# Rows scattered to expert regions batch by batch, and expert output added into the residual rows, in a mixture-of-experts layer

## The chip, the cores and the metric

The kernel runs on one core of a Trainium2 chip, as one program. The metric is the time on the device in microseconds. Two times are told apart: that of unprofiled runs (their median), and the span of one execution taken by the hardware profiler, on which every row of a view is placed.

## What is computed

The input is x of 8 x 1024 tokens with 256 features, in float32. Two blocks follow one another, each on a layer-normalised x and added back to x:

```
x = x + layernorm(block1(layernorm(x)))     # per-token attention between heads, then an MLP
x = x + layernorm(block2(layernorm(x)))
# block2, on rows h: causal attention with 16 heads over the 1024 tokens of a batch, then
h      = clip(h + attention @ Wo, -100, 100)
flat   = rmsnorm(h, ln2_w)                             # 8192 rows of 256
probs  = softmax(flat @ Wr)                            # 8 experts
topv, topi = top_k(probs, 2);  topv = topv / sum(topv)
o_e    = (silu(flat @ Wg[e]) * (flat @ Wu[e])) @ Wd[e] # Wg, Wu: 256 x 512, Wd: 512 x 256
out    = clip(h + sum over the two experts of topv * o_e, -100, 100)
```

## The kernel before

The program has two parts. `attention_kernel` (lines 83 to 1271) runs a loop of eight iterations, one for each batch, on all engines at once. Tokens are in tiles of 128 rows, 8 tiles to a batch (NT), 64 in all (TT). A batch has three phases; at the end every engine counts itself in (`end_batch`, line 293), SP clears all semaphores one by one (line 360) and lets the four engines go.

- In phase 1, Pool forms for each tile the outer products of keys and values (`work<-QK,VS`, line 434, two halves for a tile), PE sums them over the heads (line 1070), ACT copies the sums to KVS, and DVE (13 heads) and Pool (3 heads, `q_share`, line 397) multiply them with the queries (line 207); DVE reduces (lines 815 and 818). Then the MLP, the layer norms and the rotary embedding. Pool's list of work is fixed: products of tile t, share of tile t - 1, gain of tile t - 3 (`gain2`, line 423). After phase 1 Pool has nothing more to do in the batch.
- In phase 2 there are the scores, the maxima and the weighted values of the attention.
- In the last phase DVE forms H2 (the residual rows) and FL (= flat, in the tile AT), PE the router's logits, and DVE finds the two best experts of each token with `max` and `max_index` (line 1004) and puts expert numbers and shares into ROUTE (lines 1007 to 1015). SP stores x1 (the residual of the second addition, line 340), h2 (line 352), flat (354) and route (356), the latter behind the semaphore `topk`, and waits for all of them before it clears the semaphores.

`experts_kernel` (line 1274) has three blocks, each closed by a barrier of the engines.

- `route_tokens` (1296) loads the routes of all tokens and the 12 MB of expert weights (line 1334). Counts and running sums give each (token, choice) pair a slot; the slots of an expert are padded to whole tiles, 136 tiles in all. Then 64 x 2 pairs of one-hot matrices, made on DVE (lines 1411 to 1413) and multiplied on PE (line 1435), turn the slots into `source`, the list of the tokens in each tile, and `texp` holds the expert of each tile.
- `run_experts` (1444) loops over the 136 tiles, eight to an iteration. Pool gathers 128 rows of flat with an indirect DMA (1498) up to four tiles ahead; PE turns the tile (1575), does the two projections (1584), turns the gated activations (1611) and projects down (1620). ACT does silu and two evacuations (1526, 1531, 1542), DVE the gate (1554) and the copy of the result to Y (1567), and SP stores Y to scratch_y in slot order (1488). DN is one PSUM bank, Y has two buffers.
- `combine` (1626) works in 16 blocks of four tiles. For each, SP loads x1 and h2, Pool gathers the two expert rows of every token (8 indirect DMAs, line 1688) by the slots, DVE multiplies by the shares and adds (1726), clips (1729), takes the statistics (1732, 1736), ACT the root and the normalisation (1704, 1707), DVE adds x1 (1744), and SP stores the output.

A `Signal` counts what was signalled so far; `settle` waits for that count.

## Time and profile before

| | us |
|---|---|
| median of 3 runs | 4459.59 (4457.14 to 4460.53) |
| span of the profiled execution | 4458.2 |
| batches (8) | 0 to 3330.2 |
| routing | 3330.2 to 3457.2 |
| expert loop | 3457.2 to 4251.7 |
| combination | 4251.7 to 4458.2 |

| engine | busy us | share |
|---|---|---|
| PE | 3281.8 | 74% |
| DVE | 2525.6 | 57% |
| ACT | 1616.7 | 36% |
| POOL | 1256.7 | 28% |

The busy shares are means over stages with different limits, so the page alone doesn't say what bounds the kernel. The slices show where the stages are, the windows give each stage's own busy times, and the timeline shows who releases whom. In a row of the timeline, the part in brackets is the engine's idle time before it and what ended it. Times of issue and landing of DMAs are in a view of their own.

### The profile page before, as it was taken

The page shows a single profiled execution, that of the slowest core. Times are in us where ns is not written, and L with a number is a line of the kernel's source. Part 1 is how long each engine was busy: PE and PEld are TensorE (multiplying, and loading weights), DVE is VectorE, ACT ScalarE, POOL GpSimd, SP SyncE. Part 2 cuts the span into 40 slices and gives each one's busy share as a digit, 9 for nine tenths or more (in the row PEclk, how much of TensorE's full clock was granted, in tenths as well). Part 3 has the DMA queues.
Part 4 walks back from the last instruction along what each step waited for, and adds up shares of the span by engine and source line. Part 5 has one row for each costly group of instructions (what it writes and reads, how often), then busy time and mean ns, then how long its engine had stood idle before and what let it go on. Part 6 is the DMA issues. An engine that isn't in the chain of part 4 may idle for free. (4 is left out here: it accounts for less than half of the span.)

```text
span 4458.2 us, 53612 instructions
## 1 busy us (share of the span) xinstructions
PE 3281.8 (74%) x17032; PEld 1909.6 (43%) x17033; DVE 2525.6 (57%) x4655; ACT 1616.7 (36%) x3717; POOL 1256.7 (28%) x873
## 2 busy tenths in 40 slices
PE   6667859775977687587759775976774999999910
PEld 5433623452354235333623452453331666666600
DVE  6764857386658656673857486566749111111156
ACT  2435245433634352444236333624440222222222
POOL 6400910271055008201810460064000111111156
PEclk9889979887988798798879887987885999999955
DMA  1130040004000400310040004002212111111156
GB/s 31 21 52 21 1 71 3 21 0 73 2 20 11 63 21 1 48 25 21 1 72 2 20 1 73 2 20 36 28 45 90 47 45 45 45 45 45 43 182 199
DMA packets 172478, 177.41 MB, mean 40 GB/s; under 512 B 31952, under 2 KB 159696, under 8 KB 172240
## 3 DMA queue, kind: packets, MB, share of 16 engines
q1 hardware_dynamic: 159568, 139.78, 14.6%
q0 software_dynamic: 12672, 34.62, 2.6%
q8 instruction: 130, 2.13, 0.2%
q14 instruction: 108, 0.88, 0.1%
HBM read 106.32 MB, written 67.24 MB: 39 GB/s over the span
## 5 line engine op out<-in xcount | busy, mean ns | idle before, releaser
L434 POOL TENSOR_TENSOR work<-QK,VS 128x2048 f32<-128x2048 f32 x128 | 520.1, 4086 | 1734.7 <-DVE QK L764 1734.2
L925 DVE TENSOR_REDUCE NM<-MX 128x1 f32<-128x128 f32 (+7 forms) x1024 | 735.3, 753 | 448.8 <-PE MX L1162 438.5
L652 ACT ACTIVATE PR<-SP_ 128x512 f32<-128x512 f32 (+3 forms) x1536 | 694.0, 489 | 459.8 <-PE SP_ L1196 312.9
L1160 PE MATMUL MX<-KST,work 96*128 96x512 bf16 (+3 forms) x1536 | 444.8, 354 | 270.9 <-DMA work<-scratch_qd 211.5
L1193 PE MATMUL SP_<-work,KST 99*128 99x512 bf16 (+3 forms) x1536 | 469.6, 333 | 69.6 <-ACT PR L652 32.3
L1554 DVE TENSOR_TENSOR AG<-UB,SL 128x512 f32<-128x512 f32 x136 | 94.1, 692 | 500.3 <-PE UB L1584 500.3
L1160 PEld LDWEIGHTS MX<-KST,work 96*128 96x128 bf16 x1536 | 127.3, 103 | 534.8 <-DVE NM L925 225.5
L1209 PE MATMUL OA<-PR,V 128*32 128x512 f32 (+3 forms) x3072 | 327.3, 498 | 3.3 <-ACT PR L652 3.3
L818 DVE TENSOR_REDUCE AT<-work 128x208 f32<-128x3328 f32 x56 | 324.6, 5797 | 0.0
L1070 PE MATMUL OB<-work,ident 128*128 128x256 f32 x1024 | 258.9, 416 | 74.9 <-POOL work L434 74.9
L1531 ACT ACTIVATE SL<-GB 128x512 f32<-128x512 f32 x136 | 81.3, 598 | 602.6 <-PE GB L1584 602.6
L1193 PEld LDWEIGHTS SP_<-work,KST 99*128 99x128 bf16 x1536 | 145.7, 98 | 288.6 <-ACT PR L652 198.5
L1070 PE MATMUL OA<-work,ident 128*128 128x256 f32 x1024 | 238.2, 392 | 40.9 <-POOL work L434 40.9
L1498 POOL DMA_INDIRECT XG<-scratch_flat,index x136 | 129.4, 952 | 492.5 <-PE TX L1575 457.2
L1070 PEld LDWEIGHTS OB<-work,ident 128*128 128x128 f32 x1024 | 212.8, 211 | 119.6 <-issue 83.6
L207 DVE TENSOR_TENSOR work<-QK,KVS 128x3328 f32<-128x3328 f32 x64 | 263.5, 4117 | 0.0
L1584 PE MATMUL GB<-wg,XTm 128*128 x544 | 257.8, 596 | 0.3 <-issue 0.3
L1620 PE MATMUL DN<-wd,AGT 128*128 x1088 | 257.1, 379 | 0.8 <-ACT AGT L1542 0.8
L1584 PE MATMUL UB<-wu,XTm 128*128 x544 | 256.0, 593 | 0.0
L1620 PEld LDWEIGHTS DN<-wd,AGT 128*128 128x128 f32 x1088 | 206.6, 190 | 86.6 <-issue 65.5
L1162 PE MATMUL MX<-mask_qk,identb 128*128 128x128 bf16 x1024 | 236.5, 233 | 0.0
L1070 PEld LDWEIGHTS OA<-work,ident 128*128 128x128 f32 x1024 | 196.3, 195 | 81.0 <-issue 43.4
(242 smaller groups left out, 5252.7 us busy)
## 6 DMA issues: line engine op xcount, KB each, us to landing
work<-scratch_qd SPq DMA_DIRECT2D x96, 256.0 KB, 9.4
scratch_y<-Y SPq DMA_DIRECT2D x136, 128.0 KB, 1.7
scratch_qd<-work SPq DMA_DIRECT2D x48, 256.0 KB, 7.7
X<-in_L_attn_x SPq DMA_DIRECT2D x8, 1024.0 KB, 5.7
scratch_x<-X SPq DMA_DIRECT2D x8, 1024.0 KB, 16.2
scratch_h<-A SPq DMA_DIRECT2D x8, 1024.0 KB, 4.6
scratch_flat<-AT SPq DMA_DIRECT2D x8, 1024.0 KB, 6.2
XH<-scratch_x SPq DMA_DIRECT2D x16, 512.0 KB, 4.3
```

Of the source, the lines that this page charges most:

```text
L207: return eng.tensor_tensor(dst.rearrange("p (h e d) -> p h e d", e=HD, d=HD), QK[:, u % 3, h0 * HD:h1 * HD].rearrange("p (h e) -> p h e", ...
L434: sg["prod1"].by(pool.tensor_tensor(P1[t % 2][:, i * hh * D:(i + 1) * hh * D].rearrange("p (h e d) -> p h e d", h=hh, e=HD), QK[:, t % 3, ...
L652: sg["exp"].by(act.activation(PR[:, n % 8, q0:512], SP_[:, n % 2, q0:512], ACT.Exp))
L818: sg["attn"].by(dve.tensor_reduce(AT[:, u, 0:c0].rearrange("p (h d) -> p h d", d=HD), P2[:, 0:(H - POOL_HEADS) * D].rearrange("p (h e d) - ...
L925: sg["mx"].by(dve.tensor_reduce(NM[:, qt, h:h + 1], src, AX.X, ALU.max, negate=True))
L1070: m = pe.matmul(OAB(u)[:, 0:D], ident[:, :], P1[u % 2][:, h * D:(h + 1) * D], start=h == 0, stop=h == H - 1)
L1160: m = pe.matmul(out, lhsT, KST[0:MROW, g, k0:k1], start=True, stop=not last)
L1162: m = pe.matmul(out[:, k1 - k0 - P:k1 - k0], identb[:, :], mask_qk[:, :], start=False, stop=True)
L1193: m = pe.matmul(SP_[:, n % 2, q0:512], KST[0:KROWS, g, kt * P:(kt + 1) * P], QST[0:KROWS, g * G + h, c * 512 + q0:(c + 1) * 512], start=Tr ...
L1209: m = pe.matmul(OA[32 * h:32 * (h + 1), q0:512], V1[:, kt, g, :], PR[:, (G * k + h) % 8, q0:512], start=kt == 0, stop=last, tile_position= ...
L1584: m = pe.matmul(out[:, s % 2], XT[:, s % 2, c * P:(c + 1) * P], w[:, bass.ds(e, 1), c, :].squeeze(1), start=c == 0, stop=c == FC - 1)
L1620: m = pe.matmul(DN[:, 0:D], AGT[:, s % 2, c * P:(c + 1) * P], wd[:, bass.ds(e, 1), c, :].squeeze(1), start=c == 0, stop=c == FK - 1)
```

## The change

The route and flat tensors in DRAM, the lists, the gathers and the scratch_y tensor go. The parts:

1. FL becomes the first 256 columns of a tile FX with rows of 260 values: the row, the number of the first choice, the difference of the two shares, the second share, and the row's number in h2. FX, SLOT and `count` live through both parts of the program. x1 and h2 are laid out so that a partition's rows are contiguous in DRAM; h2 has 128 spare rows.
2. At the end of each batch, DVE builds the one-hots of the two choices, PE sums them with two float32 matmuls of 64 columns, and DVE forms each pair's row in a DRAM tensor xs with a region for each expert, and keeps the running count. The store of the route and that of flat go.
3. At the start of the next batch Pool issues 16 indirect DMAs that scatter the rows of FX (1040 bytes each) to xs, ahead of its other work. In the first iteration they write to spare rows. DVE waits for them before it writes FL again. The scatters of the last batch stand in the routing block.
4. `plan_tiles` takes the place of `route_tokens`: from the eight counts it forms the expert and the first row of each tile, and SP writes 128 padding rows behind each region.
5. In `run_experts`, SP loads each tile with a plain DMA whose row comes from a register, four tiles ahead. DVE works out each row's share from the row itself and multiplies it in with the evacuation. Pool adds the tile to h2 with an indirect DMA that accumulates, and waits for each before the next. x1 is loaded into SBUF in 16 pieces meanwhile.
6. `finish` takes the place of `combine`: no gathers; h2 in blocks of four tiles with four buffers, the clip on Pool, and two blocks between statistics and addition on DVE.

The setup uses a part of `work` for the raw weights and has 12 more Pool instructions and one more DMA.

```
             with pool.Fori(0, B) as b:
+                for t in range(NT):
+                    for j in range(2):
+                        pool.indirect_dma_start(
+                            out=dram["xs"], out_offset=bass.IndirectOffsetOnAxis(ap=SLOT[:, j, t:t + 1], axis=0),
+                            in_=FX[:, t, :], in_offset=None).then_inc(scattered, 16)
...
-                sp.wait_ge(sg["fl"].sem, NT)
-                st_.by(sp.dma_start(fld[bass.ds(b, 1)].squeeze(0), FL[:, :, :]), 16)
-                sp.wait_ge(sg["topk"].sem, 1)
-                st_.by(sp.dma_start(routed[bass.ds(b, 1)].squeeze(0), ROUTE[:, :, :]), 16)
...
+                    if c == 0:
+                        dve.wait_ge(scattered, (b + 1) * (2 * 16 * NT))
...
+                for j in range(2):
+                    ds.by(dve.tensor_tensor(M[:, j], ioe[:, :].unsqueeze(1).broadcast_to(sh),
+                                            topi[:, :, j:j + 1].broadcast_to(sh), ALU.is_equal))
+                sg["onehot"].by(dve.tensor_tensor(BR[:, :, :], M[:, 0], M[:, 1], ALU.add))
...
+                dve.wait_ge(sg["sums"].sem, 1)
+                ds.by(dve.tensor_copy(tot[:, :, :], MX[:, 1, 1, 0:NT * E].rearrange("p (t e) -> p e t", e=E)))
+                ds.by(dve.tensor_tensor_scan(cum[:, :, :].rearrange("p e t -> p (e t)"), ...
...
+                sg["slots"].by(dve.tensor_copy(SLOT[:, :, :], slotf[:, :, :]))
...
+                pe.wait_ge(sg["onehot"].sem, 1)
+                pe.matmul(MX[:, 1, 0, 0:NT * E], below[:, :], choices, start=True, stop=True)
+                sg["sums"].by(pe.matmul(MX[:, 1, 1, 0:NT * E], ones[:, :], choices, start=True, stop=True))
...
 (plan_tiles, SP and Pool)
+            sp.wait_ge(sg["const"].sem, 5)
+            sp.wait_ge(sg["ends"].sem, 1)
+            for e in range(E):
+                row = sp.value_load(endi[0:1, e:e + 1], min_val=0, max_val=E * REGION)
+                sg["padded"].by(sp.dma_start(dram["xs"][bass.ds(row, P), :], pad[:, :]), 16)
+            sg["padded"].settle(sp)
...
+            for t in range(NT):
+                for j in range(2):
+                    sg["scattered"].by(pool.indirect_dma_start(... in_=FX[:, t, :] ...), 16)
...
 (run_experts, SP, Pool and DVE)
+            def load(s, n):
+                row = sp.value_load(at, min_val=0, max_val=E * REGION)
+                sp.dma_start(XG[:, s], dram["xs"][bass.ds(row, P), :]).then_inc(sg[f"loaded{s}"].sem, 16)
...
+                    pool.wait_ge(sg["y"].sem, n0 + s + 1 + CREDIT)
+                    if not (first and s == 0):
+                        pool.wait_ge(sg["added"].sem, (n0 + s) * 16)
+                        pool.sem_inc(sg["freed"].sem, 1)
+                    pool.indirect_dma_start(
+                        out=dram["h2"], out_offset=bass.IndirectOffsetOnAxis(ap=XG[:, s, ROW - 1:ROW].bitcast(U32), axis=0),
+                        in_=Y[:, s % 2], in_offset=None, compute_op=ALU.add).then_inc(sg["added"].sem, 16)
...
-                    dve.tensor_copy(Y[:, s % 2], DN[:, 0:D]).then_inc(sg["y"].sem, 1)
+                    dve.wait_ge(sg["freed"].sem, n0 + s - 1 + AHEAD)
+                    dve.tensor_scalar(Y[:, s % 2], DN[:, 0:D], share[:, s, 1:2], None, ALU.mult).then_inc(sg["y"].sem, 1)
...
 (finish)
+            for n in range(NB):
+                sp.wait_ge(sg["out"].sem, (n + 1) * U)
+                sg[f"stored{n % R}"].by(sp.dma_start(od[n], X1[:, n * U:(n + 1) * U, :]), 16)
+                if n + R < NB:
+                    load(n + R)
...
+            for n in range(NB):
+                pool.wait_ge(sg[f"loaded{n % R}"].sem, 16 * (n // R + 1))
+                sg["clip"].by(pool.tensor_scalar(h, h, 100.0, -100.0, ALU.min, ALU.max))
```

## Rows read from the trace of the kernel before

**Rows 1.** The page's slices: mean busy share of the DMA engines, in tenths.

```profile
DMA  1130040004000400310040004002212111111156
```

**Rows 2.** Windows: us, busy time and count by engine, granted PE clock, DMA share, GB/s.

```profile
454.00:563.30 109.30, 89.12 (x356) 70.19 (x356) 93.72 (x46) 24.58 (x68) 102.44 (x32) 0.92 0.00 1
3330.20:3372.00 41.80, 11.74 (x24) 3.25 (x24) 30.10 (x94) 0.00 (x0) 1.45 (x8) 0.50 0.97 304
3372.00:3457.20 85.20, 45.60 (x114) 11.82 (x113) 78.09 (x326) 0.67 (x2) 4.36 (x6) 0.50 0.02 5
3457.20:4251.70 794.50, 793.28 (x2988) 495.05 (x2988) 151.84 (x272) 186.14 (x408) 131.36 (x164) 1.00 0.14 44
4251.70:4458.20 206.50, 0.00 (x0) 0.00 (x0) 128.52 (x402) 48.24 (x88) 133.34 (x160) 0.51 0.64 204
```

**Rows 3.** Timeline, end of the first batch: start, duration, engine, line, out<-in, idle before.

```profile
432.30 0.18 DVE L1007 CAST ROUTE<-topi 128x16 f32<-128x16 uint32 x1
...
433.13 0.17 DVE L1015 TENSOR_TENSOR ROUTE<-tw 128x8 f32<-128x8 f32 x1
```

**Rows 4.** SP's semaphore clears, by source line 360.

```profile
L360 SPq EVENT_SEMAPHORE_RANGE_CLEAR  x736: 25/30/49, 436.6 to 3329.4; - x184
```

**Rows 5.** Timeline, start of the second batch.

```profile
444.83 1.28 ACT L486 ACT_TABLE_LOAD   x1 [12.25 <-issue]
...
454.00 14.54 POOL L434 TENSOR_TENSOR work<-QK,VS 128x2048 f32<-128x2048 f32 x4 [240.48 <-DVE QK L764]
...
468.50 1.50 POOL L207 TENSOR_TENSOR PP<-QK,KVS 128x768 f32<-128x768 f32 x1
...
469.93 3.62 DVE L207 TENSOR_TENSOR work<-QK,KVS 128x3328 f32<-128x3328 f32 x1
```

**Rows 6.** First batch: Pool by source line 434, and its first product in the timeline.

```profile
L434 POOLq MODIFY_POOL_CONFIG  x16: 11/11/11, 24.3 to 2920.5; - x16
...
39.53 7.29 POOL L434 TENSOR_TENSOR work<-QK,VS 128x2048 f32<-128x2048 f32 x2 [32.76 <-DVE QK L764]
```

**Rows 7.** Timeline of the combination, Pool's gathers.

```profile
4256.32 0.95 POOL L1688 DMA_INDIRECT Y<-scratch_y,indexc  x1 [0.30 <-issue]
...
4361.87 1.26 POOL L1688 DMA_INDIRECT Y<-scratch_y,indexc  x1 [0.30 <-issue]
```

**Rows 8.** DMA issues: kernel's tensors, count, KB each, median us to landing.

```profile
scratch_y<-Y SPq DMA_DIRECT2D x136, 128.0 KB, 1.7
...
XH<-scratch_h SPq DMA_DIRECT2D x16, 512.0 KB, 5.5
...
wd<-in_L_ffn_Wd SPq DMA_DIRECT2D x1, 4096.0 KB, 32.1
...
XG<-scratch_flat,index POOLq DMA_INDIRECT x136, 2.7
Y<-scratch_y,indexc POOLq DMA_INDIRECT x128, 3.3
```

**Rows 9.** Timeline, start of the expert loop.

```profile
3455.01 0.69 PE L1575 MATMUL TX<-identm,XG 128*128 128x128 f32 x2 [5.42 <-DMA XG<-scratch_flat,index]
...
3457.17 3.62 PE L1584 MATMUL GB<-wg,XTm 128*128 x4 [0.29 <-issue]
```

**Rows 10.** Timeline, one tile of the expert loop.

```profile
3481.94 0.38 PE L1575 MATMUL TX<-identm,XG 128*128 128x128 f32 x2
...
3483.14 0.94 POOL L1498 DMA_INDIRECT XG<-scratch_flat,index  x1 [4.41 <-PE TX L1575]
```

**Rows 11.** Combination grouped by line: count, busy us, mean ns, idle before.

```profile
L1744 DVE TENSOR_TENSOR XH<-XH 128x256 f32<-128x256 f32 x64 | 27.2, 425 | 13.9 <-ACT XH L1707 10.7
L1732 DVE BATCH_NORM_STATS2 stc<-XH 128x6 f32<-128x256 f32 x64 | 22.5, 414 | 0.5
...
L1736 DVE BATCH_NORM_AGGREGATE mvc<-stc 128x2 f32<-128x6 f32 x64 | 6.1, 157 | 2.4 <-DVE stc L1732 0.5
```

**Rows 12.** Timeline of Pool in phase 1 of the second batch.

```profile
494.23 4.11 POOL L423 TENSOR_TENSOR A<-AT,g2row 128x256 f32<-128x256 f32 x1
```

More of the change, by code:

```diff
@@ L1387, in _ @@
[L1387 to L1393 removed]
+            do(dve.memset(eps[:, :], LN_EPS))
@@ L1416, in _ @@
-            one_hots(0, True)
-            with dve.Fori(1, TT - 1) as t:
-                one_hots(t)
-            one_hots(TT - 1)
-            dve.wait_ge(sg["lists"].sem, 2 * TT)
-            do(dve.tensor_copy(src[:, :, :], pk[:, 0:2 * NS].rearrange("p (x n) -> p x n", x=2)))
-            do(dve.scalar_tensor_tensor(out=src[:, 0], in0=src[:, 1], scalar=float(P), in1=src[:, 0], op0=ALU.mult, op1=ALU.add))
-            do(dve.tensor_copy(source[:, :], src[:, 0]))
-        @block.tensor
-        def _(pe):
-            pe.wait_ge(sg["onehot"].sem, 1)
-            choices = BR[:, :, :].rearrange("p t e -> p (t e)")
-            pe.matmul(pr[:, 0:TT * E], below[:, :], choices, start=True, stop=True)
-            sg["sums"].by(pe.matmul(pt[:, 0:TT * E], ones[:, :], choices, start=True, stop=True))
-            def lists(t, first=False, last=False):
-                for j in range(2):
-                    pe.wait_ge(sg["place"].sem, 2 * t + j + 1)
-                    pe.matmul(pk[:, 0:2 * NS], lane1[:, j], tile1[:, j].rearrange("p x n -> p (x n)"),
-                              start=first and j == 0, stop=last and j == 1).then_inc(sg["lists"].sem, 1)
-            lists(0, first=True)
-            with pe.Fori(1, TT - 1) as t:
-                lists(t)
-            lists(TT - 1, last=True)
@@ L1466, in run_experts @@
         DN = ps("DN", [P, 512])
-        sg = Signals(nc, ctx, "index gathered0 gathered1 gathered2 gathered3 tx xT g gu silu ag tpa agT down y stored0 stored1 moved", "m_")
+        names = "tx xT g gu silu ag tpa agT down y picked share added freed " + " ".join(f"loaded{s}" for s in range(UNROLL))
+        sg = Signals(nc, ctx, names, "m_")
         N = NSLOT_TILES
         U = UNROLL
-        yd = dram["y"]
         block = ctx.enter_context(nc.Block())
@@ L1522, in _ @@
+            pool.sem_inc(sg["freed"].sem, AHEAD)
+            body(0, True)
+            with pool.Fori(1, N // U) as i:
+                body(i * U, False)
+            pool.wait_ge(sg["added"].sem, N * 16)
         @block.scalar
@@ L1644, in combine @@
-        rows = {n: dram[n].rearrange("(i t p) f -> i p t f", t=U, p=P) for n in ("x1", "h2")}
+        HH = sb("HH", [P, R, U, D])
+        st = sb("stc", [P, R, U, 6])
+        mv = sb("mvc", [P, R, U, 2])
+        cf = sb("cfc", [P, R, 3, U])
+        sg = Signals(nc, ctx, "clip stat var std inverse shift norm out " + " ".join(f"loaded{r} stored{r}" for r in range(R)), "c_")
+        hd = dram["h2"][0:B * S].rearrange("(p g) f -> p g f", p=P)
         od = out.rearrange("b (i t p) f -> (b i) p t f", t=U, p=P)
```

433 lines of the change are left out of this document (203 added, 230 removed).

## The prediction

> **What bounds the kernel now.** I read the row of DMA shares in the page's slices first [rows 1], then cut the span into stages by the windows view [rows 2], and then read the two ends of a batch in the timeline [rows 3 to 6]. Eight batches take 0 to 3330 us. Token routing takes 3330.2 to 3457.2: at first the DMA engines are full with the expert weights (share 0.97), then they are idle and a chain on DVE and PE builds the lists. The expert loop takes 3457.2 to 4251.7 with PE busy 793.3 of 794.5 us at full clock: it is bound by PE alone. The combination takes 206.5 us with no PE work; what it waits for is Pool, which issues 128 gathers one after another [rows 7]. In the first phase of a batch both Pool (102.4 of 109.3 us) and DVE (93.7) are nearly full [rows 2], so this phase starts its chain when Pool starts.
>
> I sum in profiled time, span 4458.2 us. The median is 4459.6, so 1.4 us are added at the end. A change within 0.2% (8.9 us) counts as none.
>
> **Routing stage: 70 us less.** The scans over 64 tiles, 128 pairs of one-hots and the list matmuls go. What is late next is the load of the weights. The windows put its end at 3372, 41.8 us after the stage begins (DMA share 0.97 up to there, 0.02 behind it [rows 2]; wd, the last, needs 32.1 us to land [rows 8]). Now 16 scatters of the last batch (2.1 MB) run beside these 12.6 MB; at the window's 304 GB/s [rows 2] they add 7 us, 0 to 7 as bounds, so about 48. The 8 padding rows sit behind the weights on SP's queue; two landings of about 2 us and a block change bring the first tile's load, and from a tile's landing to the first GB matmul it is 2.2 us (PE turns the first tile at 3455.01, GB starts at 3457.17 [rows 9]). Pads 2, block change 1, four loads issued and the first landed 3, then 2.2: the first GB comes 57 us after the stage begins, against 127.0 now. The scatters on Pool (16 at 1.25 us [rows 7], 20 us) and the short DVE plan behind them lie under the weights; without that cover they would cost about 30 us. Gain 70; bounds 60 to 78 (pads that are not held up by the weights).
>
> **Expert loop: nothing, if the scatter-add keeps up.** PE's work for a tile is unchanged, 794.5 us for 136 tiles or 5.84 us each [rows 2]. Two DVE instructions on one column are added beside 5.8 us in which DVE works 1.1 us; the product with the share takes the place of a PSUM copy of equal size; SP loads tiles four ahead (23 us of cover), and the pieces of x1 fill an idle queue (DMA share 0.14 [rows 2]). The open price is Pool's. Each tile is added to h2 by one indirect DMA, and Pool waits for its landing before it issues the next; behind this wait stand the release of Y, so the next Y product and the next DN matmul. No accumulating DMA is in the trace. Bounds: a wait released at 3482.32 (end of TX) leads to an issue at 3483.14, 0.8 us [rows 10]; a gather lands 2.7 us after its issue, 3.3 in the loaded stage, a plain store of 128 KB 1.7 [rows 8]. The lower end is 0.8 + 1.7 = 2.5 us. The upper end doubles a loaded gather and a store in sequence, as if each row were read, added and written in turn: 0.8 + 2 x (3.3 + 1.7) = 10.8. I take one loaded gather and half a store more, 0.8 + 3.3 + 0.9 = 5.0 us, nearer to the gather, which has the same 128 rows and the same issuer. That is 0.8 us below the tile's 5.84, so the loop keeps its 794.5 us. The margin is thin.
>
> The Trainium skill (DMA: Bandwidth & Descriptors, Anatomy of one DMA — SWDGE path) gives a DMA from Pool some 2.0 us fixed, most of it the receipt of the write, plus bytes at 436 GB/s; with one more read of the row the landing would be estimated at about 3.6 us with the instruction's 0.95, and the loop would stay PE-bound with more room. Our gather's 2.7 agrees with the fixed part; no run shows the accumulating form.
>
> **End: 104 us less.** Now the stage from the last Y to the end is 206.5 us [rows 2], paced by 8 gathers per block of four tiles at 1.25 us and more [rows 7]. After: the last scatter-add must land (0.8 + 4.2) and the block changes (2.2 as now), 7.2. A first load of 512 KB lands in 5.5 us [rows 8]; the clip moves to Pool, priced by a Pool instruction with two inputs and 768 columns at 1.50 us [rows 5], so 2.0 for 1024 columns with one input. DVE then does 16 blocks: four statistics 1.41 and four additions 1.70 (22.5 and 27.2 us for 64 [rows 11]), aggregation 0.38 (6.1 us for 64), and root, inverse and shift, three operations in turn on ACT and DVE, some 0.7 together (0.17 to 0.2 each as in [rows 3], and the passing on), 4.2 us in all; Pool and DVE slow each other (256 columns took 4.11 us on Pool beside DVE's product, [rows 12]), so I take 5.0, bounds 4.2 and 7.0. 16 x 5.0 = 80. The last normalisation and addition 4, the last store 3.4. Sum 7.2 + 5.5 + 2.0 + 80 + 4 + 3.4 = 102, gain 104, bounds 72 to 117. The transfers are 16.8 MB; at 304 GB/s 55 us, so they are hidden, just.
>
> The Trainium skill (GPSIMD Engine Reference, Key points) says that GpSimd shares its SBUF interfaces with VectorE and contends with DVE instructions that have two SBUF inputs. The additions here are such; a clip held through each of them would be 3.7 us and still under the 5.0, so the sum would be the same by either.
>
> **Start of each batch: 87 us more.** The scatter of the previous batch stands first in Pool's loop, before the products of tile 0, and is queued ahead of them. The cores are let go at 444.8; Pool's first product starts at 454.00, released by DVE [rows 5], so Pool has 9.2 us of slack. Sixteen indirect DMAs at the 1.25 us of back-to-back gathers [rows 7] take 20.0, and 0.8 to start: Pool is free at 465.6, 11.6 us late. Does this reach the end of the phase? Pool works without a gap from 454.00 on, DVE's first attended product waits until 469.93 for a row of work that begins with Pool's product, and after it DVE is full as well [rows 2, 5]. I find no slack, so the whole 11.6 goes on the path, 7 times: 81. In batch 0 Pool is free at 24.3 and needed at 39.5 [rows 6]: 24.3 + 20.8 = 45.1, 5.6 more. Together 87; bounds 48 (0.95 each, without the 0.30 between) and 127 (1.56 each, as beside DVE [rows 7]).
>
> **End of each batch: 7 us more.** The store of the route and its landing leave the path: DVE's last operation ends at 433.30, the clears start at 436.6 [rows 3, 4], 3.3 us. Against it DVE gets 16 more small operations, from 5 to 21. Five took 1.0 us [rows 3]; some 14 dependent steps at 0.20 to 0.26 and the rest overlapped give 4.9, while PE's two sums of 64 columns lie beside DVE's work on the shares. So +3.9 - 3.3 = +0.6, and two more semaphores of 92 that take 8.2 us to clear, +0.2: +0.8, 8 times 7; bounds -4 and +24. The stores of flat and x1, the setup's extra Pool operations (about 5 us, before PE's start at 16) and FL inside rows of 260 cost nothing: each ends long before what waits for it.
>
> **The sum.** 4458.2 - 70 + 0 - 104 + 87 + 7 = 4378 us, and 1.4 around it: 4380 us, 1.8% less.
>
> **Rivals.** (1) Slower: the scatter-add takes longer than a tile. Then the loop is paced by Pool's wait. With a landing of 6.5 us the chain is 7.3 and the loop costs 136 x 1.46 = 199 more: 4579. It turns the sign from a chain of 5.84 + 80/136 = 6.4 us. For it: the whole operation is absent from the trace and its upper bound is 10.8; against it: the small landings of both of its halves. (2) The scatter at the batch start is hidden, because PE and ACT have work of the next tiles to do meanwhile: 4380 - 87 = 4293. Against it stand the gapless rows of Pool and DVE. (3) Scatters on Pool cost more than gathers, 2 us each, as rows of 1040 bytes: 8 x 16 x 0.75 = 96 more, 4476, slower by 0.4%; nothing in the trace points there. (4) Pool's clip paces the end at 7 us a block: 32 more, 4412, inside my forecast's own range.
>
> **How the numbers follow.** Forecast with its own bounds (4330 to 4440) 0.70, rival 1 0.17, rival 2 0.08, rival 3 0.05. Faster 0.78 (the forecast and rival 2), same 0.04 and slower 0.18 (rivals 1 and 3, a part of them near zero). The range: low 4325, which leaves out rival 2; high 4475, which takes in rival 3 and the mild end of rival 1.
>
> **What would show it.** Scatter-add: the tiles' pace on PE's GB rows stays about 5.8, and Pool waits for DVE's Y, not for a DMA. Batch start: Pool's first product about 21 us after the release, DVE's first attended product 11 to 12 us later than now, and batches some 12 us longer. Routing: first GB 57 us after the stage begins, behind the weights. End: 5 us from block to block, DVE the busiest. I am wrong if the GB pace is above 5.9, if a batch grows by under 8 or over 18 us, or if the last stage takes over 125.

## The result and the profile after

| | us |
|---|---|
| before, median of 4 runs on one chip | 4460.06 (4457.14 to 4463.38) |
| after, median of 4 runs | 4350.69 (4344.27 to 4355.95) |
| ratio | 0.9757, 95% interval 0.9745 to 0.9769 |
| span of the profiled execution, before and after | 4458.2 and 4343.7 |

The changed kernel is 2.4% faster: 109.4 us in the medians, 114.5 us in the spans. Forecast were 4380 us and 1.8%. By stages of the two spans (a stage is taken from the issue of the first weight to the first GB matmul, from there to the last DN matmul, and from there to the end):

| | before | after | difference | forecast |
|---|---|---|---|---|
| batches | 3330.7 | 3409.5 | +78.8 | +94 |
| routing | 126.5 | 50.7 | -75.8 | -70 |
| expert loop | 794.1 | 795.2 | +1.1 | 0 |
| end | 207.0 | 88.3 | -118.7 | -104 |

The windows of the kernel after, to be read beside those of [rows 2] (us, busy time and count of PE, weight loads, DVE, ACT and Pool, granted PE clock, DMA share, GB/s). The first is phase 1 of the second batch from Pool's first product on, then the weights, the expert loop and the end:

```profile
471.79:581.09 109.30, 86.20 (x346) 68.08 (x346) 92.28 (x42) 21.55 (x60) 102.28 (x32) 0.90 0.01 2
3409.51:3451.40 41.89, 0.00 (x0) 0.00 (x0) 8.12 (x19) 0.00 (x0) 16.53 (x22) 0.50 1.00 360
3460.23:4255.44 795.21, 794.45 (x2988) 495.59 (x2988) 194.38 (x543) 186.19 (x408) 210.63 (x135) 1.00 0.32 55
4255.44:4343.70 88.26, 0.01 (x1) 0.00 (x0) 59.08 (x225) 37.47 (x81) 18.22 (x17) 0.51 0.61 193
```

Phase 1 has the same 102.3 us of Pool in 109.3 as before: it is not slower, it is later. The loop is still PE's, 794.45 of 795.21 us at full clock. In the end stage DVE has 59.1 us instead of 128.5.

**A batch's end and start.** The timeline from the last step that both kernels share (`tw`, 432.19 before, 440.28 here) over the last slot number and SP's clears to the second batch (start, duration, engine, line, out<-in, idle before; the row of clears is the view of source line 373):

```profile
440.28 0.15 DVE L1041 TENSOR_TENSOR tw<-top 128x8 f32<-128x8 f32 x1
...
444.48 0.17 DVE L1084 CAST SLOT<-slotf 128x16 uint32<-128x16 f32 x1
...
L373 SPq EVENT_SEMAPHORE_RANGE_CLEAR  x752: 25/30/49, 444.8 to 3407.5; - x188
...
451.60 1.00 POOL L426 DMA_INDIRECT scratch_xs<-FX,SLOT  x1 [232.64 <-issue]
452.84 1.28 ACT L520 ACT_TABLE_LOAD   x1 [12.16 <-issue]
...
471.79 3.68 POOL L468 TENSOR_TENSOR work<-QK,VS 128x2048 f32<-128x2048 f32 x1
```

From `tw` to ACT's release it is 12.56 us, and 12.64 before (432.19 to 444.83 [rows 5]). Slots take DVE until 444.65, where before it ended at 433.30 [rows 3] and SP then waited for the store of the route until 436.6 [rows 4]. From ACT's release to Pool's first product it is 18.95 us, 9.17 before [rows 5]: 9.8 more. DVE's first attended product starts 36.5 us behind the release (489.32), 25.1 before (469.93 [rows 5]). Over the batches 2 to 8 the mean distance of Pool's first products is 423.57 us, 413.20 before.

**Routing.** The stage begins at 3409.51 with the issue of the first weight. Behind it on SP's queue, and the first PE work of the expert loop:

```profile
3416.84 13.47 SPq L1397 DMA_DIRECT2D wd<-in_L_ffn_Wd  x1
3432.17 21.06 SPq L1403 DMA_DIRECT2D scratch_xs<-pad  x8
3456.08 8.79 SPq L1505 DMA_DIRECT2D XG<-scratch_xs  x8
...
3458.14 0.69 PE L1598 MATMUL TX<-identm,XG 128*128 128x128 f32 x2 [59.01 <-DMA XG<-scratch_xs]
...
3460.23 3.78 PE L1607 MATMUL GB<-wg,XTm 128*128 x4 [0.28 <-issue]
```

The weights have landed at 3451.4, 41.9 us after the first issue, as before, although 2.1 MB of scatters ran beside them: the second window above shows share 1.00 and 360 GB/s, against 304 [rows 2]. From there it is 4.7 us to the issue of the first tile's load (3456.08), 2.1 to PE's first transpose and 2.1 to the first GB.

**Expert loop.** Pool's scatter-add by source line 1527 (count: duration in ns min/median/max, its idle time by what ended it, landing), and one tile's Y with Pool behind it in the timeline:

```profile
L1527 POOL DMA_INDIRECT scratch_h<-Y,XG x136: 1556/1561/1637, 3473.4 to 4258.2; - x136
  DVE Y L1590: 522.4, 115
  DMA scratch_h<-Y,XG: 78.1, 18
DMA to landing us min/median/max: 3.6/3.8/5.5
...
3507.52 0.48 DVE L1590 TENSOR_SCALAR Y<-DN,share 128x256 f32<-128x256 f32 x1 [1.06 <-PE DN L1643]
...
3508.82 1.56 POOL L1527 DMA_INDIRECT scratch_h<-Y,XG  x1 [3.75 <-DVE Y L1590]
```

Pool waits for DVE's Y 115 times of 136 and 18 times for its own last DMA. GB follows GB at 5.82 us (median), and with the changes from one expert to the next the loop takes 5.85 us a tile.

**End.** The last scatter-add, the first clip and the statistics behind it, one block further on, and the waits of the stage (us in total, times, longest):

```profile
4258.22 1.56 POOL L1527 DMA_INDIRECT scratch_h<-Y,XG  x1 [2.98 <-DMA scratch_h<-Y,XG]
4268.04 1.04 POOL L1687 TENSOR_SCALAR HH<-HH 128x1024 f32<-128x1024 f32 x1 [8.26 <-DMA HH<-scratch_h]
4269.18 1.41 DVE L1712 BATCH_NORM_STATS2 stc<-HH 128x6 f32<-128x256 f32 x4 [13.21 <-POOL HH L1687]
...
4326.31 1.04 POOL L1687 TENSOR_SCALAR HH<-HH 128x1024 f32<-128x1024 f32 x1 [3.56 <-DMA HH<-scratch_h]
4326.38 0.99 DVE L1725 SCALAR_TENSOR_TENSOR cfc<-mvc,cfc 128x4 f32<-128x4 f32 x1
...
4331.61 1.40 DVE L1712 BATCH_NORM_STATS2 stc<-HH 128x6 f32<-128x256 f32 x4
...
POOL HH L1687 <- DMA HH<-scratch_h: 55.1, 16, 9.4
```

The statistics of the 16 blocks start at 4269.18 to 4331.61, 4.16 us apart in the mean. Pool waits for a load before every clip.

### The profile page after: what moved, and what is told of

Same layout as the page of the kernel before. It is cut to its first block and busy times, and to the rows that moved or that the text cites. A ratio compares the mean times of both kernels' runs of the same rounds, so it can differ in the third digit from the quotient of the medians.

```text
span 4343.7 us, 52684 instructions
## 1 busy us (share of the span) xinstructions
PE 3234.6 (74%) x16932; PEld 1905.7 (44%) x16933; DVE 2419.9 (56%) x4478; ACT 1605.2 (37%) x3710; POOL 1358.4 (31%) x849
## 5 line engine op out<-in xcount | busy, mean ns | idle before, releaser
L426 POOL DMA_INDIRECT scratch_xs<-FX,SLOT x128 | 124.0, 969 | 1678.3 <-issue 1678.0
L1527 POOL DMA_INDIRECT scratch_h<-Y,XG x136 | 212.2, 1560 | 616.2 <-DVE Y L1590 522.4
L1140 PE MATMUL OA<-work,ident 128*128 128x256 f32 x1024 | 252.7, 409 | 105.4 <-POOL work L468 105.4
L1140 PEld LDWEIGHTS OA<-work,ident 128*128 128x128 f32 x1024 | 207.2, 206 | 149.6 <-POOL work L468 81.4
```

What stands on the lines that cost most here:

```text
L1140: m = pe.matmul(OAB(u)[:, 0:D], ident[:, :], P1[u % 2][:, h * D:(h + 1) * D], start=h == 0, stop=h == H - 1)
L1527: pool.indirect_dma_start(out=dram["h2"], out_offset=bass.IndirectOffsetOnAxis(ap=XG[:, s, ROW - 1:ROW].bitcast(U32), axis=0), in_=Y[:, s ...
```

## The experiments

Where the time of a changed kernel is given without an interval, it is that of one execution. The kernel before took 4447.4 to 4473.1 us in seven executions on one chip, so differences of half a percent between such times aren't told apart, and the smaller effects are read from the stages and rows of the traces.

### Where the 16 scatters stand

Theory A was that the 10 us in each batch are Pool's queue and nothing else. From the start of its last gain (line 452) to the start of the rotary embedding it is 34.8 us, nearly all of it idle for Pool, and Pool is idle throughout phase 2. So the scatters were moved into these gaps.

```
             with pool.Fori(0, B) as b:
-                (the 16 scatters)
                 ...
                 sg["ag"].settle(pool)
+                (the 16 scatters)
                 for t in range(NT):
                     pool.wait_ge(sg["q2"].sem, t + 1)
```

> Pool issues the same 16 scatters of the previous batch, not ahead of its products but after its last gain, where it stood idle for 34 us in each batch of the kernel before. Nothing is left out. Theory A (the scatters at the start of a batch push the whole phase 1): Pool's first product comes some 10 us earlier again in each of seven batches and 6.6 us in the first, so the span falls by 70 to 80 us from 4343.7 to about 4268, and the batch period goes back from 423.6 to about 413.5. Rival B (the longer batch comes from the longer end of a batch and the store of the rows, wherever the scatters stand): the period stays above 420 and the span above 4320. Rival C (the scatters hurt DVE or the rotary products where they now stand): period between 415 and 420.

Measured: 4349.53 us, ratio to before 0.9753 (0.9728 to 0.9778), the same as the changed kernel, and not the 4268 of theory A. A batch takes 424.1 us. The start of the batch was free again, yet all of it was lost elsewhere. ACT in the second batch, behind Pool's first scatter of that batch (the last starts at 589.62):

```profile
570.49 0.99 POOL L479 DMA_INDIRECT scratch_xs<-FX,SLOT  x1 [0.28 <-POOL A L452]
...
587.43 0.38 ACT L575 ACTIVATE A2T<-SP_ 128x256 f32<-128x256 f32 x1 [7.44 <-remote]
...
590.92 0.38 ACT L575 ACTIVATE A2T<-SP_ 128x256 f32<-128x256 f32 x1 [3.11 <-remote]
```

PE had ended the transposes that these copies wait for by 584.2 and 588.6. The release reached ACT some 3 and 2 us later, too late for the view to name PE as the releaser ("remote"). Such rows are in every batch, 22 on ACT (79.3 us of idle in all, not all of it delay) and 2 on DVE; the traces of before and after have none. From the last gain to the rotary embedding it is now 43.5 us, 8.7 more. TensorE's clock doesn't begin it. The granted clock is at 1.2 GHz (0.50) for 10.2 us of this stretch, from 587.9 on, where with eight and eight it is at 2.4 GHz; but the first late release of the batch comes before that, at 585.31.

The second run left eight scatters at the start and put eight in the gap:

```
-                for t in range(NT):
+                for t in range(NT // 2):
                     (two scatters, at the start)
                 ...
                 sg["ag"].settle(pool)
+                for t in range(NT // 2, NT):
+                    (two scatters)
```

> Eight of the 16 scatters stand at the start of a batch, eight after Pool's last gain. Nothing is left out. Theory A with a slack: eight take 8 x 1.28 = 10.2 us from Pool's release, which came 1.2 us before ACT's, and Pool's product was needed 9.2 us after ACT's release, 10.4 after its own: the eight fit into the slack, and the period is that with none at the start, 413 to 414, span 4265 to 4275. Rival (each scatter at the start costs its 1.28 us, without slack): the saving is half, period about 418.5, span about 4305.

Measured: 4270.17 us, span 4268.3, a batch 413.9 us. In the second batch:

```profile
449.59 0.97 POOL L426 DMA_INDIRECT scratch_xs<-FX,SLOT  x1 [0.30 <-issue]
451.46 14.53 POOL L468 TENSOR_TENSOR work<-QK,VS 128x2048 f32<-128x2048 f32 x4 [0.90 <-issue]
```

Pool ends its eighth scatter at 450.56, and DVE its operand QK at 451.37, so the product doesn't wait for Pool. The first half of the scatters fits in the slack and the second half in the gap; 75.6 us of the 78.8 by which the batches had become longer are gone (3409.5 and 3333.9). Theory A holds for the start. What was slow with 16 in the gap is a second cost.

### What delays PE's release of ACT

Two runs took apart what the 16 scatters in the gap had and the eight had not: to run beside the transposes of the second half of the MLP (P), or to be many on end (N).

```
 (16 in the gap, a pause until the copies are done)
                 for t in range(NT):
+                    if t == NT // 2:
+                        pool.wait_ge(sg["a2T"].sem, NT)
                     (two scatters)
```

> All 16 scatters stand in the gap before the rotary embedding, but Pool waits after the eighth until ACT has copied the last tile of A2T. In the run with 16 in the gap without this pause, ACT's second group of A2T copies (line 575) came 7.4 and 3.1 us after it was idle, released late, and the batch took 424.1 us, where eight in the gap gave 413.9. Theory P (what is slow is PE's hand-over of these transposes while scatters are in flight): the copies come as in the run with eight, 4.0 and 0.3 us of idle, the batch takes 413 to 415 us and the span is 4260 to 4275. Theory N (it is the number of scatters issued on end, the eleventh and later ones): the pause is of no use or the late releases move to the lines that run beside scatters 9 to 16; a batch takes 420 to 424 us, span 4320 to 4348.

```
 (eight at the start, eight in the gap, but later)
                 sg["ag"].settle(pool)
+                pool.wait_ge(sg["hid"].sem, 1)
                 for t in range(NT // 2, NT):
                     (two scatters)
```

> Eight scatters at the start of the batch and eight in the gap, as in the run of 4270.17 us, but Pool waits with those in the gap until PE has done the first half of the MLP's first product (the semaphore hid), so that they run beside the second group of A2T copies instead of before it. Theory P (PE's transposes hand over late while scatters are in flight): the idle time before these copies grows from 4.0 to 6 or 7 us and from 0.3 to 2 or 3, and a batch takes 418 to 424 us, span 4300 to 4350. Theory N (the number of scatters on end): eight are too few, so the batch stays at 413 to 415 us and the span at 4265 to 4280.

Measured: 4287.79 and 4278.62 us with 4471.54 for one execution of before on that chip (0.959 and 0.957; 0.957 was the ratio of the run with eight and eight). A batch takes 415.5 and 414.5 us. In the later variant the scatters run from 574.22 to 584.10, and ACT's second group of copies lies within them:

```profile
578.58 0.66 ACT L580 ACTIVATE A2T<-SP_ 128x256 f32<-128x256 f32 x2 [4.03 <-PE SP_ L1112]
```

No late release, so P falls: scatters beside these transposes are not enough. With the pause there is no "remote" row either; the copies came before the ninth scatter. But seven releases by PE are 0.6 to 0.7 us late there, six of them to DVE with all second eight issued, one to a copy in the last batch. In the second batch PE ends OB at 592.72 (as a rule the release comes 0.04 us later in this phase), and:

```profile
593.33 0.42 DVE L890 TENSOR_TENSOR O<-OB,A 128x256 f32<-128x256 f32 x1 [0.55 <-PE OB L1179]
```

PE's next instruction, which waits for the same matmuls, starts 0.64 us behind them too. So here eight on end were not wholly without effect. Open was whether a short pause does as well, so in a third run the second eight go beside the copies, behind a pause only as long as the first eight need to land.

```
                     if t == NT // 2:
+                        pool.wait_ge(scattered, (b + 1) * (2 * 16 * NT) - 16 * NT)
+                        pool.sem_inc(sg["drained"].sem, 1)
```

> All 16 scatters in the gap before the rotary embedding, with a short pause: after the eighth, Pool waits until all that it has issued have landed (2 to 3 us), and then issues the other eight, which so run beside the second group of A2T copies. What is to be told apart is what made ACT's copies late in the run with 16 scatters on end, and not where eight ran beside the same copies, nor where Pool paused until these copies were done. Theory D (scatters on end pile something up, and a short pause drains it): no copy is late, 4.0 and 0.3 us of idle before the second group, a batch takes 413 to 417 us, 4270 to 4295. Theory T (the second eight within some 20 us of the first are enough, with or without a short pause): idle of 6 to 8 and 2 to 3 us before these copies, a batch takes 420 to 424 us, 4320 to 4350.

Measured: 4272.05 us, before 4461.9 on that chip, 414.0 us for a batch.

```profile
574.02 0.95 POOL L482 DMA_INDIRECT scratch_xs<-FX,SLOT  x1 [2.28 <-DMA scratch_xs<-FX,SLOT]
...
575.51 0.66 ACT L578 ACTIVATE A2T<-SP_ 128x256 f32<-128x256 f32 x2 [4.03 <-PE SP_ L1110]
576.48 0.66 ACT L578 ACTIVATE A2T<-SP_ 128x256 f32<-128x256 f32 x2 [0.32 <-PE SP_ L1110]
```

A pause of 2.3 us takes all late releases away, and the time with them: theory D's number, though from one execution. How far it proves D has a limit. With 16 on end the first late release of this batch was due when PE ended OB at 583.76, 13.3 us after the first scatter and with 11 of them issued; it reached DVE (line 888) at 585.31. Here the copies were released on time up to 576.48, 14.7 us after the first scatter, but with ten issued. So the time since the first scatter is not the cause; that an eleventh after the pause would have been harmful can't be excluded, because until 587 us ACT and DVE wait for PE no more. What is shown is that in this gap eight on end cost at most the 0.7 us above, that 16 on end cost 8.7 us a batch, and that the same 16 with a pause of 2.3 or 5.6 us in the middle cost little or nothing (0.957 and 0.959 of before, eight and eight 0.957).

That 16 on end are enough by themselves is not so, and the changed kernel shows it. At the start of the second batch its scatters run on end from 451.60, the twelfth starts at 465.69, and yet:

```profile
464.35 1.03 PE L1129 MATMUL MX<-wqkvT,XT 128*128 128x256 f32 x4
...
465.42 0.60 ACT L598 ACTIVATE EX<-MX 128x512 f32<-128x512 f32 x1 [3.12 <-PE MX L1129]
```

PE ends at 465.38 and ACT has its release 0.04 us later. In the seven batches 1 to 7 there is one such release each with 11 to 14 scatters issued, 13.5 to 17.1 us behind the first, and all are on time. So something in the gap of phase 1 is needed besides the number. What it is, and what piles up, no run shows; a scatter lands in 2.5 us (median), so few are under way at a time.

### All 16 in phase 2

```
                 end_phase(pool, 1)
+                (the 16 scatters; none at the start of the batch)
                 end_phase(pool, 2)
```

> All 16 scatters of a batch stand at Pool's start of phase 2, in which Pool has nothing else to do; none at the start of the batch and none before the rotary embedding. Here SP also moves queries and keys through DRAM (DMA share 0.7 over the first 60 us of the phase). Theory A (only Pool's queue at the start of the batch costs something): 4260 to 4275 us. Theory P (PE's transposes hand over late while scatters are in flight; phase 2 has none of that kind): the same, 4260 to 4275. Theory N (scatters beyond the tenth on end delay any release by PE): in phase 2 ACT and PE hand over to each other every half microsecond, so 9 us or more in each batch, 4330 to 4400. A rival of another kind: the 2.1 MB of scatters delay the queries' transfers, which phase 2 waits for (26 us of waits on them in each batch before), by up to 5 us in each batch: 4300 to 4310.

Measured: 4318.10 us, span 4316.2, a batch 420.3 us. Waits of the second batch's phase 2, first of this run, then of the run with eight and eight (us in total, times, longest):

```profile
DVE NM L960 <- PE MX L1233: 61.5, 46, 18.5
PE MX L1231 <- DMA work<-scratch_qd: 31.3, 2, 18.1
```

```profile
DVE NM L965 <- PE MX L1238: 55.0, 44, 15.4
PE MX L1236 <- DMA work<-scratch_qd: 25.8, 2, 13.6
```

The queries' transfers through DRAM come 5.5 us later; that is the rival of another kind, and with it most of the 6.4 us by which a batch is longer than with eight and eight (413.9) is accounted for. Late releases are there too, but few (three of DVE in all batches, 3.0 us, 19.9 to 21.8 us after the first scatter), and cost little, for PE starts its scores 12 us into the scatters and DVE is behind it. Theory A's 4260 to 4275 falls for this place: Pool's gap is free, the DMA engines are not.

### The price of the scatter-add

The loop costs nothing as long as the chain of Pool fits under a tile. One run doubled the operation (each adds half of Y), one took the addition out of it, so that in that one the expert rows overwrite the residual rows.

```
-                    pool.indirect_dma_start(out=dram["h2"], ..., in_=Y[:, s % 2], compute_op=ALU.add)
+                    for k in range(2):
+                        if k:
+                            pool.wait_ge(sg["added"].sem, (n0 + s) * 32 + 16)
+                            pool.sem_inc(sg["turned"].sem, 1)
+                        pool.indirect_dma_start(out=dram["h2"], ..., in_=Y[:, s % 2], compute_op=ALU.add)
```

> Each tile of the expert loop is added to h2 twice, one after the other with a wait for the landing between, each time with half the share; the sum is the same. It doubles the chain of waits on Pool: landing 3.8 us and about 0.7 from the wait to the next issue, so one link is 4.5 and two are 9.0 us a tile. Theory (the scatter-add sets the pace as soon as its chain is longer than PE's 5.85 us): loop of 136 tiles at about 9.0 us, 1225 us in place of 796, span about 4773; Pool waits for its own DMA in each tile. Rival (the accumulating DMAs overlap or the chain hides behind the four tiles of lookahead): loop below 900 us.

Measured: 4838.28 us; forecast were 4773, from links of 4.5 us. By source line 1531:

```profile
L1531 POOL DMA_INDIRECT scratch_h<-Y,XG x272: 1556/1560/1636, 3473.4 to 4749.2; - x136
  DMA scratch_h<-Y,XG: 767.8, 245
```

```profile
3606.68 1.56 POOL L1531 DMA_INDIRECT scratch_h<-Y,XG  x1 [3.05 <-DMA scratch_h<-Y,XG]
3611.24 1.56 POOL L1531 DMA_INDIRECT scratch_h<-Y,XG  x1 [3.01 <-DMA scratch_h<-Y,XG]
```

Now Pool waits for its own DMA nearly always, and one link of the chain is 4.6 us from issue to issue: 3.8 to land and 0.8 to go on. The loop takes 1270.0 us, 9.34 a tile, twice 4.6 and a little; the last stage takes 105.9 us instead of 88.3. So the single chain is 4.6 us under PE's 5.85: 1.2 us of margin, and rival 1's mechanism is real, only its price is not.

```
-                        in_=Y[:, s % 2], in_offset=None, compute_op=ALU.add)
+                        in_=Y[:, s % 2], in_offset=None)
```

> The indirect DMA of the expert loop writes the rows of Y over h2 in place of adding them; what is left out is the addition, so the output holds the expert part of one expert alone. It measures what the accumulating form costs: with it Pool's instruction takes 1.56 us and the landing 3.8. I expect 0.97 us and 2.5 us, as for the scatters to the regions, and no change of the time: PE sets the pace of 5.85 us in both. Rival (the accumulate loads the DMA engines and slows the tile loads or the matmuls): the loop gets shorter by more than 3 us.

Measured: 4345.79 us, span 4343.9, the loop 795.2 us as with the addition. Without it the instruction takes 0.96 us instead of 1.56 and lands in 2.6 us instead of 3.8: the addition costs 0.6 us of Pool and 1.2 us of landing, and nothing here.

### What the missing gathers gave

The kernel before, whose combination gathers for its first two blocks alone:

```
-            with pool.Fori(1, NP) as i:
-                for k in range(2):
-                    gather(i, k)
...
-                    dve.wait_ge(sg[f"gathered{k}"].sem, (i + 1) * 32 * U)
+                    dve.wait_ge(sg[f"gathered{k}"].sem, 32 * U)
```

> The kernel before, whose combination gathers the expert rows for its first two blocks alone; the other 14 blocks add the rows of those two, so that the expert part of the output is left out there. All the rest of the combination stays: loads, shares, clip, statistics, stores. Theory A (Pool's 128 gathers pace the last stage): without them DVE does, with 128.5 us of busy time in it: the stage falls from 206.5 to 135 to 150 us and the time to 4388 to 4404. Rival: the stage is bound by its loads and stores (share 0.64 of the DMA engines) or by the steps in turn of DVE and ACT, and keeps 190 us or more: 4440 or more. In the first case the new form of the addition (87.7 us) would owe some 60 us of its 119 to the missing gathers and the rest to DVE's work that went, in the second nearly all to the order of the blocks.

Measured: 4436.79 us; its last stage takes 175.5 us instead of 207.0, between the two theories. The window of that stage:

```profile
4259.51:4435.00 175.49, 0.00 (x0) 0.00 (x0) 128.49 (x402) 48.24 (x88) 16.24 (x20) 0.51 0.47 156
```

Here block follows block at 9.4 us on DVE (4303.69 and 4313.13 for the start of line 1741), of which it works 8.0 (128.49 / 16). So Pool's gathers did end last in the kernel before, but DVE stood only 2 us a block behind them: 31.5 of the 118.7 us belong to the gathers. DVE's own work fell by 69.4 us (128.49 to 59.08), and the remaining 17.8 are idle time of DVE. That the order with two blocks between statistics and addition closed it is argued: no run changes the order alone.

### The padding rows, and five buffers

```
-            (SP) the eight stores of pad behind the weights
 (Pool) the constants ahead of the last batch's 16 scatters, no longer behind them
+        @block.scalar
+        def _(act):
+            act.wait_ge(sg["const"].sem, 5)
+            act.wait_ge(sg["ends"].sem, 1)
+            for e in range(E):
+                row = act.value_load(endi[0:1, e:e + 1], min_val=0, max_val=E * REGION)
+                sg["padded"].by(act.dma_start(dram["xs"][bass.ds(row, P), :], pad[:, :]), 16)
```

> The changed kernel with the eight stores of the padding rows issued from ACT's queue instead of SP's, where one issue was held for 13.4 us behind the expert weights. Theory A (the pads behind the weights set the first tile's load): in the changed kernel wd lands 41.9 us after the stage begins, the last pad is issued at 43.4, the first tile's load at 46.6 and the first GB matmul comes at 50.7. From ACT's queue the pads land under the weights, so the first load follows the weights alone: the first GB 44 to 47 us after the stage begins, the time 4344 to 4348, 3 to 7 less. Rival: ACT's issue is held just as SP's was, since the DMA engines are full with 12 MB, and the pads land no earlier than before: 50 to 51 us, 4350.

Measured: 4338.49 us, span 4336.6.

```profile
3406.47 8.57 ACTq L1424 DMA_DIRECT2D scratch_xs<-pad  x8
...
3412.67 17.60 SPq L1397 DMA_DIRECT2D wd<-in_L_ffn_Wd  x1
3434.64 19.10 SPq L1508 DMA_DIRECT2D XG<-scratch_xs  x8
...
3453.18 3.77 PE L1610 MATMUL GB<-wg,XTm 128*128 x4 [0.29 <-ACT XTm L1543]
```

The stage begins at 3404.60, so the first GB comes 48.6 us after it, 2.1 less. ACT's queue issued all eight in 8.6 us while SP's issues of wu (3405.06 to 3412.62) and wd were held, so the rival falls. The gain is less than expected since the first XG load is itself behind the weights now: the load stage is the weights' alone. The rest of the 7 us lies in the batches (3404.6 against 3409.5), which this edit doesn't touch. The constants had to move ahead of Pool's scatters, since the padding rows are among them, and DVE's plan starts earlier for it; the two parts of the edit aren't told apart.

Then eight and eight together with these padding rows:

> The changed kernel with both improvements: eight of the 16 scatters of a batch at the start and eight before the rotary embedding, and the padding rows stored from ACT's queue. If the two add up: 4270.2 of the first alone less 2.1 us of the second (the first GB matmul came 48.6 us after the stage began instead of 50.7): 4268, that is 0.957 of the kernel before. Rival: the pads' early landing gives nothing because eight scatters of the last batch meet them, as in the changed kernel, and the weights end the stage: 4270, no difference.

Measured: 4277.42 us (4270.70 to 4280.53) against 4461.90, ratio 0.9577 (0.9558 to 0.9595). The first GB comes 47.7 us after the stage begins, against 51.4 with eight and eight alone (3385.3 - 3333.9), so the two add up there. That the time isn't below 4270 comes from the batches: 415.6 us each instead of 413.9 on another chip, some at 413 and some at 417 to 418. The long ones lose 3.4 us between Pool's first product and the rotary embedding (149.0 to 149.1 us instead of 145.6); the kernel before has the same in its first batch (149.1) and not in its second (145.6). For 2.4 of the 3.4 us the traces show a cause, TensorE's clock. In every batch of these traces in which it is 37.2 to 37.4 us from Pool's last gain to the rotary embedding (34.8 as a rule), the granted clock is 1.2 GHz for 6.8 us from 22 us behind the gain on. Here is that stretch in a long batch and in the next, short one (the 0.50 and 1.00 behind Pool's part are the clock):

```profile
1419.60:1426.40 6.80, 6.06 (x14) 4.88 (x15) 3.56 (x17) 3.76 (x7) 0.00 (x0) 0.50 0.00 0
1836.50:1843.30 6.80, 5.48 (x23) 3.86 (x24) 4.86 (x23) 4.09 (x8) 0.00 (x0) 1.00 0.00 0
```

Four matmuls of OB take 1.91 us in the one and 1.03 in the other, and PE had been idle for 2.73 us just before in both; why the clock falls in one batch and not in the next stays open.

And with one more buffer for h2's rows in the end stage:

```
-        U, R = 4, 4
+        U, R = 4, 5
```

> The same with five buffers for the rows of h2 in the last stage instead of four (R = 5 in finish). Theory A (there Pool waits 55 us in all for loads of HH, because a buffer comes free only when its block is added; one more buffer lets the loads run a block further ahead): a block's pace goes from 4.4 to 3.8 us, 8 us less: 4260. Rival: the DMA engines carry 197 GB/s in this stage and the loads of one block land late for their own transfer time, whatever the number of buffers: no difference, 4268.

Measured: 4273.18 us (4267.52 to 4274.60), ratio 0.9568 (0.9548 to 0.9589), the lowest of the ratios with an interval; it overlaps that of the run before, so by the times alone the fifth buffer isn't told from none. The stage itself tells it: 83.7 us from the last DN matmul against 88.2. The theory had 8 us; and why, was not what it said. The grouped line of DVE's coefficients and the stage's window, first with four buffers, then with five:

```profile
L1734 DVE SCALAR_TENSOR_TENSOR cfc<-mvc,cfc 128x4 f32<-128x4 f32 x16 | 8.3, 518 | 0.6
4190.51:4278.70 88.19, 0.00 (x0) 0.00 (x0) 60.35 (x225) 37.47 (x81) 18.23 (x17) 0.52 0.61 193
```

```profile
L1734 DVE SCALAR_TENSOR_TENSOR cfc<-mvc,cfc 128x4 f32<-128x4 f32 x16 | 2.6, 162 | 0.6
4187.00:4270.70 83.70, 0.00 (x0) 0.00 (x0) 54.74 (x225) 37.47 (x81) 18.18 (x17) 0.52 0.64 204
```

A DVE instruction on four columns, with two inputs in SBUF, took up to 1.0 us, and 0.16 with five buffers. The end rows of the changed kernel above show the case: the instruction starts at 4326.38 and ends at 4327.37, and Pool's clip runs from 4326.31 to 4327.35. With five buffers the clips fall beside the statistics instead, and none is held. DVE's busy time falls by 5.6 us and the stage by 4.5. Pool's waits for loads fall by 7.7 (55.1 to 47.4), but DVE's waits for a clip only by 2.0 (15.2 to 13.2). From block to block it is 3.84 us in the mean instead of 4.16.

## Why the prediction was right, and where its terms were off

The forecast's signs and its main mechanisms held in all four stages, and none of the rivals came true. Its span was 34 us too high: 14.7 in the end stage, 15 in the batches, 6 in routing, against 1 the other way in the loop. All the larger errors lie on the same side, so the total isn't right by errors that cancel.

- **Routing, 70 forecast, 75.8.** The mis-sized term is the 7 us for the scatters beside the weights. It took the mean 304 GB/s of the window [rows 2] for what the engines can carry; they carried 360, and the weights landed as early as before. The scatters and the plan on DVE were hidden, as forecast. The pads and the change of block took 4.7 us and not 3 (one issue alone was held for 13.4 us, but under the weights), and the runs with ACT's queue got 2 to 4 us of it back. The terms written out in the forecast add up to 56.2 us, not to the 57 it goes on with.
- **Expert loop, 0 forecast, +1.1.** The landing was put at 4.2 us and is 3.8, the chain at 5.0 and is 4.6. The run with two additions shows that this chain paces the loop once it is the longer one; rival 1 had the right mechanism and a price that isn't there. The 5.0 was put together by judgement from a gather and half a store, so that it came within 0.4 us is in part luck. The estimate of 3.6 by the Trainium skill (DMA: Bandwidth & Descriptors, Anatomy of one DMA — SWDGE path) came close too, by two misses against each other: the instruction takes 1.56 us instead of the 0.95 put in there, and from its end to the landing it is 2.2 us where the estimate had 2.6. For the plain form of the same DMA that time is 1.6 us, less than the 2.0 that the Trainium skill has as fixed. Its figure comes near the trace only if the instruction is counted in it (2.6 us in all for the plain form, 2.7 for the gather).
- **End, 104 forecast, 118.7.** First statistics 13.7 us after the last DN, 14.7 forecast. The clip took 1.04 us, not 2.0: a pass over 1024 columns with one input costs less than the two-input row from which it was scaled [rows 5]. The large term is 16 blocks at 5.0; they came at 4.16 in the mean, below the lower bound of 4.2, so 13 us of the 14.7 are here. The margin for Pool and DVE slowing each other was too wide (what of it is real is 4 to 6 us in all, shown by the fifth buffer), and the lower bound was itself too high: four additions take 1.41 us in this stage, not the 1.70 of the old one. The cause given for the old stage, the gathers, was right in order and too large in share: 31.5 us are theirs.
- On the page GPSIMD Engine Reference, Key points, of the Trainium skill the forecast had feared a clip held by DVE's additions. All 16 clips take 1.04 us. The contention is there the other way: DVE's two-input instruction waits for the end of Pool's clip (0.99 us instead of 0.16).
- **Start of a batch, 87 forecast, 79.2** (7 x 10.37 and 6.6 in the first batch). The slack was taken from ACT's release. Pool is let go 1.2 us before ACT (451.60 and 452.84), where the forecast had it start 0.8 us behind, and 16 scatters take 20.2 us, so Pool comes 9.8 us late and not 11.6. The step that mattered, no slack behind it, is right: eight scatters cost nothing, sixteen cost their whole excess, and DVE's first attended product comes 11.4 us later behind the release, within the 11 to 12 of the forecast. Rival 2 (hidden by the work of the next tiles) is refuted by the 78.8 us of the batches, 75.6 of which the run with eight and eight takes away; rival 3 by the 0.97 us and 0.30 of each. The 10.37 is the whole growth of a batch, its end included.
- **End of a batch, 7 forecast, none seen.** From `tw` on DVE works for 4.4 us instead of 1.1, 3.3 more where the forecast had 3.9, and the clears follow its end at once (444.65 and 444.8) instead of 3.3 us behind it; from `tw` to the release the sum is 0.08 us shorter.

## What to carry to other kernels

A queue in front of a full phase costs exactly what exceeds the slack, so split the queued work: the part that fits in front stays, the rest goes to a gap, and a gap has to be tried for more than the issuing engine: in one here the DMA engines were taken, in the other releases came late (16 in the gap of phase 1 gave 4349.5 us, 16 in phase 2 4318.1, eight and eight 4270.2; the changed kernel took 4350.7). Price a serial chain of DMAs as landing plus restart (3.8 + 0.8 us) against the period of the engine that it follows; below it, it costs nothing, and doubled it sets the pace. When the engine that ended last is relieved, look at the second one first: the gathers at the end of this kernel hid a DVE that needed only 15% less time.

## What the runs showed of the hardware that was not expected

- With sixteen indirect DMAs on end from Pool in the gap of phase 1, releases from PE reached ACT and DVE 1.5 to 3 us late, from about the eleventh on, and a pause of 2.3 us after the eighth removed it. The same sixteen at the start of a batch delayed no release (0.04 us, with 11 to 14 issued). What makes the difference was not found.
- An accumulating indirect DMA of 128 rows of 1 KB holds Pool for 1.56 us, a plain one for 0.96, and they land in 3.8 and 2.6 us.
- DMA issues of SP were held while 12 MB were on its way (wu 6.8 us, wd 13.5, one of the pads 13.4). In the run with ACT's queue, that queue issued eight in 8.6 us while SP's wu and wd were held (7.6 and 17.6 us).
- A DVE instruction on four columns with two inputs in SBUF was held to the end of a Pool instruction that began 0.07 us earlier, 0.99 us instead of 0.16.
- The same stretch of a batch, with the same work, ran at 2.4 GHz in most batches and at 1.2 GHz for 6.8 us in some, which made it 2.4 us longer (37.2 to 37.4 us instead of 34.8, 6.8 us at a granted clock of 0.50).
